# Four transformer layers on one core: layer 0's attention hands out its key tiles in fours, with scores four ahead, eight weight buffers and another order of query chunks

## The reference, cut to what matters

```
q, k, v = xn @ w_q, xn @ w_kv          # 16 heads x 64
q, k    = rope(q), rope(k)             # first 32 features of a head turned by position
p       = softmax(mask(q @ k.T / 8))   # causal
s       = (p @ v) @ w_out
```

## Time and profile before

| | us |
|---|---|
| median of 3 runs | 5166.38 |
| lowest, highest | 5153.54, 5170.76 |
| profiled execution | 5170.1 |
| its span, first to last instruction | 5168.8 |
| PE busy over the span | 4542.4 (88%) |
| DVE, ACT, POOL busy | 3147.9, 2499.2, 2318.8 |

### The profile page before, as it was taken

How to read it: one execution, slowest core, us unless ns; L and a number is a source line. 1 busy time by engine, 2 the same in 40 slices (tenths; PEclk the granted TensorE clock), 3 DMA queues, 4 the chain that set the end, 5 groups by cost and what they waited for, 6 DMA issues and landing times. The chain is left out here.

```text
span 5168.8 us, 68806 instructions
## 1 busy us (share of the span) xinstructions
PE 4542.4 (88%) x27376; PEld 2215.6 (43%) x27376; DVE 3147.9 (61%) x4176; ACT 2499.2 (48%) x3813; POOL 2318.8 (45%) x1323
## 2 busy tenths in 40 slices
PE   5999999977886777858799999978799999999997
PEld 3444444445654333323322222224455555555554
DVE  4656565636765777752477777843465665565663
ACT  2344444436663555642266666652244444445443
POOL 0455555558771577870100000000066666666675
PEclk8999999989997999979799999988799999999998
DMA  1000000011110000000000000000000000000000
GB/s 32 3 3 3 3 3 3 3 29 32 37 28 12 2 2 2 1 5 19 3 2 2 1 2 1 1 9 1 10 3 3 3 1 3 3 3 1 3 1 9
DMA packets 61954, 36.81 MB, mean 7 GB/s; under 512 B 36308, under 2 KB 53888, under 8 KB 61376
## 3 DMA queue, kind: packets, MB, share of 16 engines
q1 hardware_dynamic: 61632, 32.41, 2.5%
HBM read 22.03 MB, written 1.05 MB: 4 GB/s over the span
## 5 line engine op out<-in xcount | busy, mean ns | idle before, releaser
L795 DVE TENSOR_REDUCE L_part<-banks 128x2 f32<-128x1024 f32 (+2 forms) x1600 | 1881.5, 1189 | 965.7 <-PE banks L646 825.0
L780 ACT ACTIVATE L_weights<-banks 128x1024 f32<-128x1024 f32 (+1 forms) x1600 | 1581.1, 1001 | 1056.4 <-PE banks L678 816.1
L704 PE MATMUL banks<-L_weights,L_V 128*32 128x512 f32 (+3 forms) x6400 | 1490.3, 602 | 3.6 <-ACT L_raw L729 1.8
L1002 POOL TENSOR_TENSOR L_wsum<-L_wsum,L_weights 128x1024 f32<-128x1024 f32 (+1 forms) x448 | 995.0, 2221 | 55.8 <-ACT L_weights L780 3.0
L985 POOL TENSOR_TENSOR L_wsum<-L_wsum,L_two 128x1024 f32<-128x1024 f32 x240 | 571.0, 2379 | 841.6 <-DVE L_two L969 838.5
L704 PEld LDWEIGHTS banks<-L_weights,L_V 128*64 128x64 f32 (+1 forms) x6400 | 282.3, 122 | 453.5 <-issue 397.0
L678 PE MATMUL banks<-L_QH,L_KH 64*128 64x512 f32 (+3 forms) x1664 | 432.0, 453 | 17.9 <-issue 10.2
L2513 POOL MEMSET F_xr<- 128x16 f32 x1 | 0.1, 127 | 933.4 <-POOLq L97 933.4
L646 PE MATMUL banks<-L_KH,L_QH 64*128 64x512 f32 (+3 forms) x1664 | 372.5, 429 | 31.7 <-ACT L_weights L780 17.5
L678 PE MATMUL banks<-L_QL,L_KH 64*128 64x512 f32 (+3 forms) x1664 | 372.0, 382 | 0.0
L678 PE MATMUL banks<-L_QH,L_KL 64*128 64x512 f32 (+3 forms) x1664 | 371.7, 381 | 0.0
(11 more groups left out here) (446 smaller groups left out, 5911.7 us busy)
## 6 DMA issues: line engine op xcount, KB each, us to landing
F_early<-F_V SPq DMA_DIRECT2D x63, 128.0 KB, 2.3
F_tab<-xpos SPq DMA_DIRECT2D x8, 512.0 KB, 4.4
F_h<-L_ffn_h_w SPq DMA_DIRECT2D x2, 1024.0 KB, 8.0
F_wqkv<-L_ffn_wqkv SPq DMA_DIRECT2D x2, 768.0 KB
L_cos<-rope_cos SPq DMA_DIRECT2D x1, 1024.0 KB, 5.0
L_sin<-rope_sin SPq DMA_DIRECT2D x1, 1024.0 KB, 7.0
out<-X SPq DMA_DIRECT2D x1, 1024.0 KB, 5.1
F_z<-F_x SPq DMA_DIRECT2D x32, 31.8 KB
```

Source lines behind the costliest of these rows:

```text
L704: mm = pe.e.matmul(O[r, c:BANK], self.V[g % 2][:, kt, h, :], self.W[x % self.NW][:, y, c:BANK], start=kt < starts, stop=kt >= tiles - starts)
L780: act.e.activation(self.W[x % self.NW][:, :, c:BANK], self.banks(it)[:, :, c:BANK], ACT.Exp, scale=self.scale).then_inc(self.exped, 1)
L795: dve.e.tensor_reduce(self.part[n % 3][:, pr, j, p, :], self.banks(it)[:, :, 0:wide], AX.X, ALU.max).then_inc(self.mx_read, 1)
L1002: pool.e.tensor_tensor(acc[:, :, c:BANK], acc[:, :, c:BANK], W[:, :, c:BANK], ALU.add).then_inc(self.summed, 1)
```

## The change

Only `RotaryAttention`, the class of layer 0's attention, sets the new switch. `FOUR` replaces `APART`; `LEAD` becomes 4 and `NW` 8. The planner now goes through the steps four at a time (`U`): four scores with the pieces spread behind them, then the shifts and the first half of the `ys`, then the values of four steps with nothing between, then the second half of the `ys`. `den` comes 4 steps after the end of a chunk, both `join`s 8 steps after it. A straight's K or Q counts as made four steps later, not two. The chunks go 2, 1, 3, 0 in the first group and 3, 0, 2, 1 in the other seven. For the other attentions `U` stays 2 and every changed expression keeps its value.

```diff
+    FOUR = False
@@ tables
-            order = list(range(4))
-            for ch in order[::-1] if self.causal and g % 2 else order:
+            order = [3, 0, 2, 1] if self.causal and g else [2, 1, 3, 0] if self.causal else list(range(4))
+            for ch in order:
@@ after
+        if self.FOUR:
+            return [(4, ("den", n)), (8, ("join", n, 0)), (8, ("join", n, 1))]
@@ plan
-        share = lambda count, left: -(-count // max(1, left // 2))
-        for x in range(0, steps, 2):
+        U = 4 if self.FOUR else 2
+        share = lambda count, left: -(-count // max(1, left // U))
+        for x in range(0, steps, U):
...
-            if x == start + 10 and g + 1 < self.groups:
+            if x == start + (8 if self.FOUR else 10) and g + 1 < self.groups:
...
-                until = self.first(4 * g + (2 if self.causal and g % 2 else 3)) - 4
+                until = self.first(4 * g + 3) - 4
...
-                take = max(share(..., self.first(m0 - 1) - 4 - self.LEAD - x) for m0 in ...)
+                take = max(share(..., self.first(m0 - 1) - 2 * U - self.LEAD - x) for m0 in ...)
...
-                made[it[1], it[2], it[3]] = x + (0 if self.EAGER else 2)
+                made[it[1], it[2], it[3]] = x + (0 if self.EAGER else U)
...
-                take = max(share(..., self.first(m0) - 2 - self.LEAD - x) for m0 in ...)
+                take = max(share(..., self.first(m0) - U - self.LEAD - x) for m0 in ...)
...
-            while shifts and shifts[0][1] < x and x >= self.first(shifts[0][0] - 1) - 2 - self.LEAD:
+            while shifts and shifts[0][1] < x and x >= self.first(shifts[0][0] - 1) - U - self.LEAD:
...
-            if self.APART:
+            if self.FOUR:
+                cut = len(ys) // 2
+                for i in range(4):
+                    items += [("score", soon + i)] if soon < steps else []
+                    items += ps[len(ps) * i // 4:len(ps) * (i + 1) // 4]
+                    items += carried if i == 0 else []
+                items += turns + eager(ys[:cut]) + [("values", x + i) for i in range(4)] + mid + eager(ys[cut:])
+            elif self.APART:
...
-            if k == self.chunk[n][2] - 2:
+            if k == self.chunk[n][2] - U:
@@ class RotaryAttention
-    APART = True
+    FOUR = True
+    LEAD, NW = 4, 8
```

More of the change, by code:

```diff
@@ L405, in plan @@
             if left:
-                take = max(share(sum(1 for m, it in left if m <= m0), self.first(m0 - 1) - 4 - self.LEAD - x) for m0 in {m for m, it in left})
+                take = max(share(sum(1 for m, it in left if m <= m0), self.first(m0 - 1) - 2 * U - self.LEAD - x) for m0 in {m for m, it in left})
                 for m, it in left[:take]:
@@ L411, in plan @@
             for it in low(ys):
-                made[it[1], it[2], it[3]] = x + (0 if self.EAGER else 2)
+                made[it[1], it[2], it[3]] = x + (0 if self.EAGER else U)
             left = [(m, it) for m, its in todo for it in its if m <= n + 2]
             if left:
-                take = max(share(sum(1 for m, it in left if m <= m0), self.first(m0) - 2 - self.LEAD - x) for m0 in {m for m, it in left})
+                take = max(share(sum(1 for m, it in left if m <= m0), self.first(m0) - U - self.LEAD - x) for m0 in {m for m, it in left})
                 for m, it in left[:take]:
```

## The result

| | before | after |
|---|---|---|
| median of 4 runs, us | 5160.23 | 5296.32 |
| lowest to highest | 5153.54 to 5170.76 | 5275.43 to 5298.20 |
| ratio, 95% interval | | 1.0247 (1.0216 to 1.0279) |
| profiled execution's span | 5168.8 | 5274.1 |

The forecast was 5230 us and a loss of 60; the loss is 136 us by the medians and 105 us between the two profiled executions. The profiled one of after is the fastest of its four.

The account below looks back on a forecast made before the run. PE's list was taken as the bound in layer 0's attention. Groups +49, last group -4, ends +9, +10, -8, -5 and clock +9 gave +60 on 5170: 5230 us, own range 5190 to 5270, 8 in 10 5110 to 5300.

Parts of the forecast that it names:

- rival D: Worse: the clock falls to 0.94, or low halves take twice as long and waits add up; 5270 to 5330 us, chance 0.15.
- sign of being wrong: PE's waits in layer 0's attention staying under 130 us, where about 190 were forecast, or pieces evenly spread.
- What grouping removes: On PE, joining four steps' values saves 36 us, first terms 7, pieces 14: together 57 us, 7 a group.
- The clock: Granted clock in layer 0's attention, with PE near 83% busy, loses one hundredth of the busy time: +9 us.
- Bank 7: Of neighbouring items in the same half, the second waits until the first is read: 11 us of PE a group.
- ScalarE's order: High halves of straights and divisions of joins ending a block delay what follows on ScalarE: 6 us a group.
- Three bank pairs: Four scores with pieces in a row make PE wait for VectorE's maxima and low halves: 12 us a group.
- A group without the clock: Period of a group near 135 us against 128.1, with a net +7 taken for each of seven groups.
- the walk through the blocks: Second way of costing a group: walking each of its ten blocks with these durations gives 133 to 135 us.
- Ends: Prologue of 12 pieces +9 us, first group's bunched pieces +10, old start's waits -8, one chunk's joins at the end -5.
- Four ahead and eight buffers: LEAD 4 and two extra weight buffers, costed at 0 because GpSimd's sums are not among PE's waits.
- Rival A: The grouping wins: waits of a group stay at about 10 us, only the 57 us count; 5113 us, chance 0.22.

Follow-up runs that it names:

- experiment 6: High halves of K and Q moved behind the next block's first exp, against the changed kernel with bank 7's items spread behind the four scores: 5166.30 us.
- experiment 1: Kernel before with the new chunk order alone, 5153.72 us; then also scores four ahead and eight buffers, steps still in twos, 5138.02 us.

## Why the prediction was right in direction and less than half in size

The measured 5296 us lie outside the forecast's own 5190 to 5270, in the range of rival D (5270 to 5330, put at 0.15), and within the range for 8 in 10. The waits came where the forecast had them, and in four fifths of its amount (152 us for about 190; under 130 would have been its sign of being wrong), so its direction is no luck. Its size is not right: PE's busy time, which was to fall by 50 to 60 us, rose by 16.

- **What grouping removes (57 us): right for the values (36), the rest a little high.** The values' busy time, all 1280 instructions, fell from 308.0 us to 268.0: 40 us for a forecast of 36 (before, then after),

```profile
L704 PE MATMUL banks<-L_weights,L_V 128*64 128x512 f32 (+3 forms) x1280 | 308.0, 560 | 0.0
```

```profile
L717 PE MATMUL banks<-L_weights,L_V 128*64 128x512 f32 (+3 forms) x1280 | 268.0, 563 | 0.0
```

  with part of them at half clock. Sixteen took 3.58 us; from the prediction's prices it is 4 x 1.01 - 3 x 0.15 = 3.59. For the whole of 57 us the sum under "The clock" leaves some 49.
- **Bank 7 (11 us a group): right.** The waits of join, den, straight and V add up to 80 us, 11.4 in each of seven groups; single ones are 1.38 (forecast 1.5 after a straight), 1.23 (1.4 after a join), 0.69 (0.7).
- **ScalarE's order (6 us a group): right,** 43 / 7 = 6.2. But in experiment 6 moving one kind of item took 24 us off these waits and nothing off the time.
- **Three bank pairs (12 us a group): too large on the wait list,** 29 / 7 = 4.2; yet with the maxima cut short the kernel is 67 us faster. Between the profiled executions its stretch is 45 us shorter, of which the wait list explains 19 (133 against 152) and the half clock, 152 - 130 = 22 us less of busy time at it, some 11; the rest stays open. All waits: 152 / 7 = 21.7 against 25 taken.
- **A group without the clock: right.** At 0.96 a group took 139 us, at 0.88 147: 8 us for 0.08. Drawn on to 1.00 that is some 135 us, and the walk through the blocks gave 133 to 135. This line is drawn through four groups; no group at full clock was measured.
- **The clock (+9 us): the step that failed.** Taken was 0.98, measured 0.92. 174 us of the stretch are at 1.2 GHz against 24 before; with PE's share of them busy (21 of 24 us) and each worth half, I estimate 150 x 0.5 x 0.87 = 65 us. The stretch grew by 102 us: PE stands idle for 154 us of it where it stood for 68 (+86), and is busy for 952 where it was for 936 (+16). With +65 for the clock in the busy time, the grouping took off 65 - 16 = 49. I read the clock off the busy share of long windows (93% gives 0.99, 79% gives 0.94) and interpolated for the mean. But the mean of a stretch does not give its clock: most of the waits lie in three blocks of ten, and around them the clock goes to half (0.74 in b4 and 0.60 in b6 of the group that ends at 717 us, 1.00 in its other eight), although the waits as a whole are no more than I thought. In rival D I had priced a fall to 0.94 at +35.
- **Ends.** The first values come 14 us later, for a forecast of +9 in the prologue. The other terms of the ends were not read out by themselves.
- **Four ahead and eight buffers (0): wrong by some 16 us,** to the good side (experiment 1). The price came from a wait list without sums of weights in it; what it brings instead is fewer waits of scores behind exp (3.5 us for 19.2) and of straights behind the copy of a shift (7.3 for 16.8).

Rival A did not happen. Its mechanism holds in part for another list: with bank 7's items spread, the stretch of the grouping by four takes 976 us, 28 less than before and 10 less than the new order with four ahead in twos. But its values start 14 us later than before, and the whole kernel, at 5154 us, is only 0.2% faster than the one before and 16 us slower than the one in twos (5138 us), far from A's 5113. That grouping by four pays in the whole time is not shown by any run.

## What to carry to other kernels

When work is batched to save mode changes, look at what shares a single buffer between the batches: an item that stands alone between two long blocks costs little, and of two side by side the second waits until the first has been read (0.7 to 1.4 us each here). Place such items between the members of the batch, and check on each engine that the reader does not end up ahead of something more urgent. What helps one list need not help another: spreading saved 142 us with values in fours and cost 37 with values in twos. And where waits come in clusters, look whether they cost twice: once as a wait, once as a clock that falls behind them, read from short windows around the cluster and not from the mean of a stage.

## What the runs showed of the hardware

- In the changed kernel the granted clock fell to half behind clusters of short waits, none over 3.0 us: 96 instructions at 0.51 for 24 us behind the joins of b5, though PE was busy for 21 of the 24 us. But the kernel with fewer waits is not always the one with the higher clock. The kernel before waits for 66 us in PE's list between first and last values and is at half clock for 24 us; with the new order alone it waits for 47 and is at half clock for 68; with four ahead and eight buffers too, for 40 and 61. Why stayed open.
- 666 more matmuls without use made the kernel 43 us faster by the medians (38 by the ratios).
- The same program's runs spread by 23 us (5275 to 5298) where the kernel before spreads by 17; in one execution, groups with the same list took 139 to 147 us.
- The best versions found, 5138 us, are 0.4 to 0.5% faster than before: the new order with scores four ahead and eight buffers, steps in twos, whether the values stand apart or in pairs.
